# A second attention whose inputs are combined by VectorE alone, with its fillings one tick later

## The chip, the core and the metric
The kernel runs on one core of a Trainium2 chip. The metric is device time in microseconds, the median of three runs. Besides those runs one execution was profiled; all rows below are from it.

## What is computed
A chain of small language-model layers over 8 sequences of 512 tokens, 256 wide: a tower of state-space layers, a window attention, a mixture of experts, a relative attention, a second mixture of experts. The change lies in the relative attention. Cut to what matters:

```python
def _L1_attn_ref(x, Wq, Wk, Wv, Wo, bo, w, v):
    q, k, val = (proj(Wq), proj(Wk), proj(Wv))          # 16 heads of 16
    R = abs(pos[:, None] - pos[None, :])
    R_hat = (1.0 + exp(vv)) / (1.0 + exp(vv - wv * R))
    scores = relu(einsum('bhqd,bhkd->bhqk', q, k)) * R_hat[None]
    scores = where(causal, -inf, scores)
    attn = softmax(scores / sqrt(hd))
    ctx = einsum('bhqk,bhkd->bhqd', attn, val)
    return ctx @ Wo + bo

h = h + _L0_ffn_ref(_layernorm(h), ...)                  # two experts' results a token, weighted
h = h + _L1_attn_ref(_layernorm(h), ...)
```

## The kernel before
The relative attention is one stage (`relative_attention_stage`). Before its own work it has to finish what the experts of the stage ahead left: each token has two result rows, read back from memory, and x must get their weighted sum. Class `Carry` (line 663) does this per sequence b: `load` (SP's queue), `halve` (ScalarE, line 698: one of the two rows times its share), `weigh` (VectorE, line 709, four instructions: the other row times its share, plus the first; line 713: that is added to the bf16 copy `xc`), and `add` (line 718: `xc` is added to x; counted in the semaphore `x_final`). `add` takes the engine as an argument. Sequence 0 is finished in the stage ahead. For sequences 1 to 7 VectorE weighs all seven in a row before the loop, and GpSimd adds each (`C.add(pool, S, b)` in the GpSimd block). The results lie in `turned` (sequences 1, 2 and 7) and in the four slots of the ring `z` (sequences 3 to 6), which the attention uses later.

The attention runs in ticks, one for each of the 8 x 16 heads; `b` is the sequence (a batch of 16 ticks), `i` the tick in it, and `h = 16 b + i`. `drive` (line 1933) writes batch 0 out, loops over batches 1 to 6, and writes batch 7 out with 9 ticks more to drain. There is no scheduler: each engine's function `tick(b, i)` fixes its order, and semaphores join the engines. In tick i:

- TensorE transposes results of earlier heads back (line 2221, in ticks with i % 4 of 3 and 0), computes the four score tiles of head h (line 2234, in the order of `ORDER` = 0, 2, 1, 3), each when VectorE has emptied that bank of the head before; transposes the masked probabilities of head h-3 (line 2246); multiplies by V for four heads at once (line 2261, in ticks with i % 4 of 3, 0 and 1); and then does at most one *filling* of the bank `psum_w` (`fill`).
- VectorE empties the four score tiles (line 2126, multiplied by `rhat`, with maxima), makes `nm` (line 2141), reads the filling of the tick before (`read`), and clamps the exponentials of head h-1 (line 2157), which GpSimd then masks (line 2007).
- ScalarE empties oT (line 2059, i % 4 of 2), reads the filling of the tick before, copies the transposed probabilities to `pt`, a view of `turned` (lines 2068, 2070), and computes the exponentials of head h (line 2076).

A filling is a step of the projections. `PRE` holds those for the next sequence (two sets of transposes "xT", four "qk" and two "v"), `POST` those of the sequence before ("cT" twice, "out" twice). The first number of an entry is its tick. `at_tick(b, i, fill)` ends TensorE's tick i, and the other engines call `at_tick(b, i - 1, read)` in the next. For "qk" ScalarE writes a rounded high part (line 2045) and VectorE the remainder, the low part `lo` (line 2107); for "out" VectorE adds the bank to x (line 2112). A filling waits in `w_free` until the one before has been read. VectorE's read frees the bank, and it stands behind all four score tiles and `nm`. SP's queue stores high and low parts to memory and loads them back as `q_st` and `k_st` for the heads.

Of the kernel before, what the change touches and what calls it, by code (L numbers as in the profile page):

```python
# [24 lines left out]
NB = 8  # L25
# [8 lines left out]
def later(n):  # L34

    return not (isinstance(n, int) and n == 0)
# [1784 lines left out]
def relative_attention_stage(nc, S, A, R, C):  # L1821
# [32 lines left out]
    with ExitStack() as ctx:  # L1854
# [66 lines left out]
        PARTS = [(0, 0), (1, 0), (0, 1), (1, 1)]  # L1921
        PRE = [(1, "xT", 0), (2, "xT", 1), (3, "qk", 0), (4, "qk", 1), (5, "qk", 2), (6, "qk", 3), (7, "v", 0), (8, "v", 1)]
        POST = [(9, "cT", 0), (10, "cT", 1), (11, "out", 0), (12, "out", 1)]

# [67 lines left out]
        def _(pool):  # L1992
            pool.memset(v_now[:, :, :, HV:HC], 0.0)
            pool.memset(vx[:, :], 1.0).then_inc(vones, 1)
            norm.pool_rstd(pool, S.minus_half, 0)
            for b in range(1, NB):
                C.add(pool, S, b)
            pool.wait_ge(loaded, 16 * 5)
# [36 lines left out]
        def _(act):  # L2035
# [17 lines left out]
            def tick(b, i):  # L2053
# [8 lines left out]
                if has(h, 3):  # L2062
                    g = h - 3
                    out = pt[:, (i - 3) % SLOTS, :, :]
                    if has(g, SLOTS):
                        act.wait_ge(o_done, g - 4 - (i - 3) % QUAD)
# [26 lines left out]
        def _(dve):  # L2093
# [24 lines left out]
            def tick(b, i):  # L2118
# [3 lines left out]
                for at, t in enumerate(ORDER):  # L2122
                    if has(h, 0):
                        n = (t + 1) * P
                        dve.wait_ge(s_done, TT * h + FILLED[at]).then_inc(passed, 1)
                        dve.tensor_tensor_reduce(out=z[:, i % RING, t, 0:n], in0=scores[t],  # L2126
                                                 in1=rhat[:, i * T + T - n:(i + 1) * T], scale=1.0, scalar=0.0,
                                                 op0=ALU.mult, op1=ALU.max, accum_out=mx[:, i % 2, t:t + 1]).then_inc(z_ready, 1)
                    half = (i - 3) % QUAD
                    if half < 2 and has(h, 11 + half):  # L2130
# [11 lines left out]
                if i == 0 and (not isinstance(b, int) or b < NB - 1):  # L2142
                    if not later(b):
                        dve.wait_ge(C.x_final, NB)
                    norm.vector_stats(dve, rows_of(b + 1), b + 1)
                if 1 <= i:
                    at_tick(b, i - 1, read)
                if i == 8 and later(b):
# [20 lines left out]
            for use, (_, kind, which) in enumerate(PRE):  # L2169
                read(kind, which, 0, use, FIRST[use])  # L2170
            for b in range(1, NB):
                C.weigh(dve, b, result_at[b])
            drive(dve, tick)
            take_ctx(NB - 1)
# [618 lines left out]
```

## Time and profile before
| | |
|---|---|
| median of 3 runs | 2643.86 us (2642.42 to 2650.0) |
| the profiled execution's own time | 2641.9 us |
| its span | 2640.2 us |
| TensorE busy | 2182.8 us (83%) |
| VectorE busy | 1586.9 us (60%) |
| ScalarE busy | 1325.2 us (50%) |
| GpSimd busy | 744.7 us (28%) |
| mean granted TensorE clock | 0.907 of full |
| relative attention | about 1591 to 2260 us of the span |

Busy shares are over all stages, which have different limits, so they say little of one change. A row of the timeline gives start, duration, engine, line, operation and what is written from what, with the number of instructions merged in it; the bracket is the idle time ahead of it and what ended it. The granted clock of TensorE is 1.00 at 2.4 GHz and 0.50 at 1.2 GHz.

### The profile page before, as it was taken

The page shows a single profiled execution, that of the slowest core. Times are in us where ns is not written, and L with a number is a line of the kernel's source. Part 1 is how long each engine was busy: PE and PEld are TensorE (multiplying, and loading weights), DVE is VectorE, ACT ScalarE, POOL GpSimd, SP SyncE. Part 2 cuts the span into 40 slices and gives each one's busy share as a digit, 9 for nine tenths or more (in the row PEclk, how much of TensorE's full clock was granted, in tenths as well). Part 3 has the DMA queues.
Part 4 walks back from the last instruction along what each step waited for, and adds up shares of the span by engine and source line. Part 5 has one row for each costly group of instructions (what it writes and reads, how often), then busy time and mean ns, then how long its engine had stood idle before and what let it go on. Part 6 is the DMA issues. An engine that isn't in the chain of part 4 may idle for free. (4 is left out here: it accounts for less than half of the span.)

```text
span 2640.2 us, 43175 instructions
## 1 busy us (share of the span) xinstructions
PE 2182.8 (83%) x13073; PEld 1686.4 (64%) x13073; DVE 1586.9 (60%) x4474; ACT 1325.2 (50%) x2652; POOL 744.7 (28%) x835
## 2 busy tenths in 40 slices
PE   3899999999999999767882873888888989695982
PEld 2788888887888888635662651555555556463772
DVE  4555665565556656356764977767777768541225
ACT  2344544454445444345545763867776768210330
POOL 5111111111111111042446662122212222226442
PEclk8899999999999999989986985988989989678996
DMA  5620010000000000022232535222122221303446
GB/s 108 166 33 0 11 33 1 8 13 24 1 8 3 1 1 0 27 65 51 43 64 68 147 109 177 78 67 64 49 70 74 71 69 51 101 33 108 127 137 243
DMA packets 209472, 165.36 MB, mean 63 GB/s; under 512 B 108320, under 2 KB 167376, under 8 KB 209296
## 3 DMA queue, kind: packets, MB, share of 16 engines
q1 hardware_dynamic: 190832, 120.71, 17.3%
q0 software_dynamic: 14240, 38.35, 4.6%
q10 hardware_dynamic: 4224, 4.19, 0.5%
q8 instruction: 81, 1.33, 0.2%
q14 instruction: 95, 0.78, 0.1%
HBM read 91.07 MB, written 72.11 MB: 62 GB/s over the span
## 5 line engine op out<-in xcount | busy, mean ns | idle before, releaser
L630 PE MATMUL psum_o<-w_s,hid_s 128*128 128x256 f32 x3072 | 384.0, 284 | 19.1 <-ACT hid L434 19.1
L616 PE MATMUL psum_h<-xn2T_s,w_s 128*128 128x512 f32 x1536 | 389.9, 404 | 5.4 <-ACT hid L434 3.6
L630 PEld LDWEIGHTS psum_o<-w_s,hid_s 128*128 128x128 f32 x3072 | 371.8, 188 | 27.0 <-issue 19.1
L433 ACT ACTIVATE hid_s<-psum_h,b 128x512 fp32r<-128x512 f32 x256 | 176.5, 689 | 391.5 <-PE psum_h L616 376.0
L616 PEld LDWEIGHTS psum_h<-xn2T_s,w_s 128*128 128x128 f32 x1536 | 283.5, 191 | 87.1 <-ACT hid L434 21.8
L2126 DVE CUSTOM_DVE_ANT_0 ra_z<-ra_psum_s,rhat 128x128 f32<-128x128 f32 (+3 forms) x512 | 224.9, 483 | 132.6 <-PE ra_psum_s L2234 120.5
L2076 ACT ACTIVATE ra_z<-ra_z,ra_nm 128x128 f32<-128x128 f32 (+3 forms) x512 | 245.4, 563 | 0.0
L2007 POOL TENSOR_SCALAR_AFFINE_SELECT ra_z<-ra_z 128x512 f32<-128x512 f32 x128 | 81.6, 637 | 477.3 <-DVE ra_z L2157 477.3
L2246 PE MATMUL ra_psum_p<-ident,ra_z 128*128 128x128 f32 x1280 | 181.4, 293 | 1.3 <-ACT turned L2068 1.3
L517 DVE TENSOR_TENSOR hid_s<-hid,hid_s 128x1024 fp32r<-128x1024 f32 x128 | 156.0, 1223 | 43.1 <-ACT hid L434 42.1
L2068 ACT ACTIVATE turned<-ra_psum_p 128x1024 f32<-128x1024 f32 x128 | 131.3, 1026 | 92.1 <-PE ra_psum_p L2246 92.1
L434 ACT ACTIVATE hid<-psum_h,b 128x512 f32<-128x512 f32 x256 | 174.4, 681 | 0.0
L2246 PEld LDWEIGHTS ra_psum_p<-ident,ra_z 128*128 128x128 f32 x1280 | 148.7, 148 | 35.8 <-issue 35.3
L117 POOL TENSOR_TENSOR ln2n_rstd<-ln2n_var_eps,minus_half 128x4 f32<-128x4 f32 x32 | 32.3, 1009 | 466.1 <-DVE ln2n_var_eps L113 466.1
L2157 DVE TENSOR_SCALAR ra_z<-ra_z,ra_em 128x128 f32<-128x128 f32 (+3 forms) x512 | 162.7, 381 | 0.0
L2234 PE MATMUL ra_psum_s<-ra_k_st,ra_q_st 48*128 48x128 f32 (+3 forms) x512 | 126.1, 367 | 43.1 <-DVE ra_mx L2126 21.2
L600 PE MATMUL psum_y<-ssm_s,xn1T_s 128*128 128x256 f32 x768 | 128.7, 305 | 13.3 <-DVE state L461 13.3
L2234 PEld LDWEIGHTS ra_psum_s<-ra_k_st,ra_q_st 48*128 48x128 f32 x512 | 80.7, 199 | 86.3 <-issue 52.5
L600 PEld LDWEIGHTS psum_y<-ssm_s,xn1T_s 128*128 128x128 f32 x768 | 106.0, 198 | 31.5 <-DVE state L461 16.2
L352 POOL TENSOR_TENSOR x<-x,b 128x1024 f32 (+1 forms) x32 | 101.2, 3162 | 82.1 <-DVE xn L123 70.7
L401 ACT ACTIVATE xn2T_s<-psum_t,ln 128x512 fp32r<-128x512 f32 x64 | 46.4, 775 | 153.5 <-PE psum_t L132 153.5
L117 POOL TENSOR_TENSOR ln1n_rstd<-ln1n_var_eps,minus_half 128x4 f32<-128x4 f32 x32 | 32.6, 1020 | 314.6 <-DVE ln1n_var_eps L113 314.6
(380 smaller groups left out, 4212.4 us busy)
## 6 DMA issues: line engine op xcount, KB each, us to landing
ex_slots<-blank SPq DMA_DIRECT2D x1, 10296.0 KB, 33.8
ex_zT<-ex_slots SPq DMA_DIRECT2D x39, 264.0 KB, 3.0
ex_rows<-ex_slots SPq DMA_DIRECT2D x8, 1056.0 KB, 9.3
w<-in_L_tok_w SPq DMA_DIRECT2D x8, 1024.0 KB, 7.5
ra_scratch<-ra_hi SPq DMA_DIRECT2D x32, 256.0 KB
ra_scratch<-ra_lo SPq DMA_DIRECT2D x32, 256.0 KB
ra_q_st<-ra_scratch SPq DMA_DIRECT2D x128, 64.0 KB, 1.8
ra_k_st<-ra_scratch SPq DMA_DIRECT2D x128, 64.0 KB, 1.8
```

Source lines behind the costliest of these rows:

```text
L433: act.activation(hid_s[:, 0, m, :], psum_h[:, m % 2, :], ACT.Gelu, bias=b1[:, m:m + 1])
L434: act.activation(hid[:, m, :], psum_h[:, m % 2, :], ACT.Gelu, bias=b1[:, m:m + 1]).then_inc(hid_ready, 1)
L517: dve.tensor_tensor(hid_s[:, 1, m:m + 2, :], hid[:, m:m + 2, :], hid_s[:, 0, m:m + 2, :].bitcast(F32), ALU.subtract).then_inc(hid_lo, 1)
L600: pe.matmul(out, xn1T_s[:, parity, x_part, k, tok], ssm_s[:, w_part, SSM_D + k * D:SSM_D + (k + 1) * D], start=(n == 0 and k == 0), stop=F ...
L616: mm = pe.matmul(psum_h[:, m % 2, :], w1_s[:, w_part, k, m * P:(m + 1) * P], xn2T_s[:, x_part, k, :], start=(n == 0 and k == 0), stop=(n = ...
L630: mm = pe.matmul(psum_o[:, t // 2, (t % 2) * D:(t % 2 + 1) * D], hid_s[:, h_part, m, t * P:(t + 1) * P], w2_s[:, w_part, m, :], start=(n = ...
L2068: act.activation(out[:, 0:8, :], psum_p[:, 0:2, :].rearrange("p c (a b) -> p (c a) b", a=4), ACT.Identity).then_inc(pt_act, 1)
L2076: act.activation(z[:, i % RING, t, 0:n], z[:, i % RING, t, 0:n], ACT.Exp, scale=SCALE, bias=nm[:, i % 2, t:t + 1]).then_inc(exp_done, 1)
L2126: dve.tensor_tensor_reduce(out=z[:, i % RING, t, 0:n], in0=scores[t], in1=rhat[:, i * T + T - n:(i + 1) * T], scale=1.0, scalar=0.0, op0=A ...
L2157: last = dve.tensor_scalar(pt_, pt_, em[:, (i - 1) % 2, t:t + 1], None, ALU.max)
L2234: pe.matmul(scores[t], q_st[64 * s:64 * s + 3 * HD, parity, t * P:(t + 1) * P], k_st[64 * s:64 * s + 3 * HD, parity, 0:n], start=True, sto ...
L2246: mm = pe.transpose(psum_p[:, c, a * P:(a + 1) * P], z[:, (i - 3) % RING, q, k * P:(k + 1) * P], S.ident[:, :])
```

## The change
Four edits in the one stage.

1. VectorE does `add` itself, right behind `weigh`, and GpSimd's additions go.
2. Only sequences 1 to 3 are combined ahead of the loop. Sequence 4 follows in tick 0, 5 in tick 1, 6 and 7 in tick 2, behind `nm` (`RESULTS_AT`). VectorE's statistics for sequence 1 wait for `x_final` 2 instead of 8; ScalarE waits for all 8 at tick 3, before it writes into `turned`, and so does VectorE.
3. All fillings stand one tick later (ticks 2 to 13 instead of 1 to 12).
4. VectorE's `at_tick(b, i - 1, read)` is called behind the second score tile, no longer behind `nm`.

```diff
-        PRE = [(1, "xT", 0), (2, "xT", 1), (3, "qk", 0), (4, "qk", 1), (5, "qk", 2), (6, "qk", 3), (7, "v", 0), (8, "v", 1)]
-        POST = [(9, "cT", 0), (10, "cT", 1), (11, "out", 0), (12, "out", 1)]
+        PRE = [(2, "xT", 0), (3, "xT", 1), (4, "qk", 0), (5, "qk", 1), (6, "qk", 2), (7, "qk", 3), (8, "v", 0), (9, "v", 1)]
+        POST = [(10, "cT", 0), (11, "cT", 1), (12, "out", 0), (13, "out", 1)]
+        RESULTS_AT = {0: (4,), 1: (5,), 2: (6, 7)}
...
             norm.pool_rstd(pool, S.minus_half, 0)
-            for b in range(1, NB):
-                C.add(pool, S, b)
             pool.wait_ge(loaded, 16 * 5)
...
                     out = pt[:, (i - 3) % SLOTS, :, :]
+                    if i == 3 and not later(b):
+                        act.wait_ge(C.x_final, NB)
...
                                                  op0=ALU.mult, op1=ALU.max, accum_out=mx[:, i % 2, t:t + 1]).then_inc(z_ready, 1)
+                    if at == 1 and 1 <= i:
+                        at_tick(b, i - 1, read)
...
                 if i == 0 and (not isinstance(b, int) or b < NB - 1):
                     if not later(b):
+                        dve.wait_ge(C.x_final, 2)
+                    norm.vector_stats(dve, rows_of(b + 1), b + 1)
+                if not later(b):
+                    for of in RESULTS_AT.get(i, ()):
+                        C.weigh(dve, of, result_at[of])
+                        C.add(dve, S, of)
+                    if i == 3:
                         dve.wait_ge(C.x_final, NB)
-                    norm.vector_stats(dve, rows_of(b + 1), b + 1)
-                if 1 <= i:
-                    at_tick(b, i - 1, read)
...
-            for b in range(1, NB):
+            for b in range(1, 4):
                 C.weigh(dve, b, result_at[b])
+                C.add(dve, S, b)
             drive(dve, tick)
```

VectorE, from the last results ahead of the loop to the first score tile of tick 0 in batch 0, before:

```order
L709 SCALAR_TENSOR_TENSOR both<-ra_z,both_share 128x256 x4
L713 TENSOR_TENSOR turned<-turned,both 128x1024
L709 SCALAR_TENSOR_TENSOR both<-turned,both_share 128x256 x4
L713 TENSOR_TENSOR turned<-turned,both 128x1024
L2126 ISA ra_z,ra_mx<-ra_psum_s,rhat 128x128
```

and VectorE in the changed kernel, behind the four tiles and `nm` of tick 0 (result 4), up to the tiles of tick 1:

```order
L2144 TENSOR_SCALAR ra_nm<-ra_mx 128x4
L106 BN_STATS ra_n_stats<-x 128x6 x4
L110 BN_AGGR ra_n_mv<-ra_n_stats 128x2 x4
L113 TENSOR_SCALAR ra_n_var_eps<-ra_n_mv 128x4
L709 SCALAR_TENSOR_TENSOR both<-ra_z,both_share 128x256 x4
L713 TENSOR_TENSOR turned<-turned,both 128x1024
L718 TENSOR_TENSOR x<-x,turned 128x1024
L123 TENSOR_SCALAR ra_xn<-x,ra_n_mv,ra_n_rstd 128x256 x4
L2127 ISA ra_z,ra_mx<-ra_psum_s,rhat 128x128
```

The last results moved from ahead of the first tile into the ticks, and each now carries its addition to x (L718).

VectorE in a tick with a low part, in the loop over batches 1 to 6, before (the clamp of the head before, L2157, follows it):

```order
L2126 ISA ra_z,ra_mx<-ra_psum_s,rhat 128x384
L2126 ISA ra_mx 128x1
L2125 REGISTER_ALU
L2126 ISA ra_z,ra_mx<-ra_psum_s,rhat 128x256
L2126 ISA ra_mx 128x1
L2125 REGISTER_ALU
L2126 ISA ra_z,ra_mx<-ra_psum_s,rhat 128x512
L2126 ISA ra_mx 128x1
L2140 ISA
L2141 TENSOR_SCALAR ra_nm<-ra_mx 128x4
L2102 REGISTER_ALU
L2107 TENSOR_TENSOR ra_lo<-ra_psum_w,ra_hi 128x512
```

and in the changed kernel, where the low part has line 2108:

```order
L2127 ISA ra_z,ra_mx<-ra_psum_s,rhat 128x128
L2127 ISA ra_mx 128x1
L2127 ISA ra_z,ra_mx<-ra_psum_s,rhat 128x384
L2127 ISA ra_mx 128x1
L2103 ISA
L2105 REGISTER_ALU
L2108 TENSOR_TENSOR ra_lo<-ra_psum_w,ra_hi 128x512
L2126 REGISTER_ALU
L2127 ISA ra_z,ra_mx<-ra_psum_s,rhat 128x256
```

The low part moved ahead of the third and fourth tile and of `nm`.

TensorE from the transposes of head h-3 to the filling of tick 3 in that loop, before (the first "qk" filling, with Wq):

```order
L2246 MATMUL ra_psum_p<-ident,ra_z 128x128 x10
L2252 ISA
L2261 MATMUL ra_psum_o<-turned,ra_v_now 32x512 x4
L2183 REGISTER_ALU
L2196 MATMUL ra_psum_w<-ra_xnT,ra_wq 128x512 x2
```

and in the changed kernel the same tick, with the second set of transposes of xn as its filling:

```order
L2254 MATMUL ra_psum_p<-ident,ra_z 128x128 x10
L2260 ISA
L2269 MATMUL ra_psum_o<-turned,ra_v_now 32x512 x4
L2191 REGISTER_ALU
L2199 MATMUL ra_psum_w<-ident,ra_xn 128x128 x4
```

The "qk" filling with Wq now ends tick 4, beside the product with V of 384 columns.

## Rows read from the trace of the kernel before

**Rows 1.** Windows (from:to, us; busy PE, PEld, DVE, ACT, POOL; PE clock; DMA; GB/s), batches 1 and 3.
```profile
1710.00:1792.70 82.70, 72.42 (x451) 46.23 (x450) 58.81 (x245) 60.20 (x131) 17.69 (x39) 0.92 0.23 67
...
1872.00:1950.90 78.90, 67.22 (x436) 43.69 (x432) 59.00 (x245) 57.76 (x128) 16.98 (x37) 0.94 0.23 67
```

**Rows 2.** VectorE in order of time (start us, us), results and first ticks.
```profile
1611.10 1.67 DVE L709 SCALAR_TENSOR_TENSOR both<-turned,both_share 128x256 bf16<-128x256 f32 x4 [0.90 <-ACT turned L698]
1612.81 0.69 DVE L713 TENSOR_TENSOR turned<-turned,both 128x1024 bf16<-128x1024 bf16 x1
1613.61 3.56 DVE L709 SCALAR_TENSOR_TENSOR both<-turned,both_share 128x256 bf16<-128x256 f32 x4
...
1639.79 0.28 DVE L2126 CUSTOM_DVE_ANT_0 ra_z<-ra_psum_s,rhat 128x128 f32<-128x128 f32 x1
...
1642.12 1.41 DVE L106 BATCH_NORM_STATS2 ra_n_stats<-x 128x6 f32<-128x256 f32 x4
...
1645.46 1.38 DVE L123 TENSOR_SCALAR ra_xn<-x,ra_n_mv,ra_n_rstd 128x256 f32<-128x256 f32 x4 [1.21 <-POOL ra_n_rstd L117]
...
1648.61 1.27 DVE L2157 TENSOR_SCALAR ra_z<-ra_z,ra_em 128x128 f32<-128x128 f32 x4
...
1653.41 0.29 DVE L2126 CUSTOM_DVE_ANT_0 ra_z<-ra_psum_s,rhat 128x128 f32<-128x128 f32 x1 [0.49 <-PE ra_psum_s L2234]
```

**Rows 3.** Instructions of line 718 and line 709.
```profile
L718 POOL TENSOR_TENSOR x<-x,turned x7: 2119/2123/2132, 1613.6 to 1640.0; 128x1024 f32<-128x1024 f32 x7
L718 DVE TENSOR_TENSOR x<-x,turned x1: 1224/1224/1224, 1589.0 to 1589.0; 128x1024 f32<-128x1024 f32 x1
...
L709 DVE SCALAR_TENSOR_TENSOR both<-ra_z,both_share x16: 471/473/2387, 1618.0 to 1634.3; 128x256 bf16<-128x256 f32 x16
```

**Rows 4.** TensorE in order of time, batch 0.
```profile
1622.77 1.51 PE L2234 MATMUL ra_psum_s<-ra_k_st,ra_q_st 48*128 48x128 f32 x4 [10.47 <-DMA ra_k_st<-ra_scratch]
...
1662.56 1.98 PE L2196 MATMUL ra_psum_w<-ra_xnT,ra_wk 128*128 128x512 f32 x4 [1.25 <-DVE ra_lo L2107]
```

**Rows 5.** Who waited for whom, 1700 to 2240 us.
```profile
PE ra_psum_w L2196 <- DVE ra_lo L2107: 15.9, 18, 1.2
...
PE ra_psum_w L2206 <- DVE x L2112: 5.0, 7, 0.7
...
PE ra_psum_w L2206 <- DVE ra_lo L2107: 2.1, 6, 0.4
```

**Rows 6.** TensorE in order of time, batch 2.
```profile
1825.35 0.90 PE L2234 MATMUL ra_psum_s<-ra_k_st,ra_q_st 48*128 48x128 f32 x4
1826.19 1.31 PE L2246 MATMUL ra_psum_p<-ident,ra_z 128*128 128x128 f32 x10
1828.72 1.98 PE L2196 MATMUL ra_psum_w<-ra_xnT,ra_wk 128*128 128x512 f32 x4 [1.23 <-DVE ra_lo L2107]
...
1857.13 1.99 PE L2206 MATMUL ra_psum_w<-ra_wo,ra_xnT 128*128 128x256 f32 x8 [0.74 <-DVE x L2112]
```

**Rows 7.** VectorE in order of time, batch 2.
```profile
1826.09 0.29 DVE L2126 CUSTOM_DVE_ANT_0 ra_z<-ra_psum_s,rhat 128x128 f32<-128x128 f32 x1 [1.52 <-PE ra_psum_s L2234]
...
1827.98 0.69 DVE L2107 TENSOR_TENSOR ra_lo<-ra_psum_w,ra_hi 128x512 fp32r<-128x512 f32 x1
...
1831.60 0.29 DVE L2126 CUSTOM_DVE_ANT_0 ra_z<-ra_psum_s,rhat 128x128 f32<-128x128 f32 x1 [1.74 <-PE ra_psum_s L2234]
```

**Rows 8.** ScalarE in order of time, batch 2.
```profile
1825.10 0.59 ACT L2059 ACTIVATE ra_oT<-ra_psum_o 128x512 f32<-128x512 f32 x1
1825.58 0.60 ACT L2045 ACTIVATE ra_hi<-ra_psum_w 128x512 fp32r<-128x512 f32 x1
...
1828.60 1.91 ACT L2076 ACTIVATE ra_z<-ra_z,ra_nm 128x128 f32<-128x128 f32 x4
```

**Rows 9.** Busy time by microsecond, batch 1, tick 6.
```profile
1746.00:1747.00 1.00, 0.08 (x1) 0.00 (x0) 0.96 (x4) 1.00 (x2) 0.00 (x0) 1.00 0.00 0
...
1748.00:1749.00 1.00, 1.00 (x2) 0.33 (x1) 0.43 (x2) 1.00 (x2) 0.40 (x1) 0.50 0.00 0
```

## The prediction

> **What bounds the kernel now.** I read the page first: span 2640.2 us, no engine full over the whole of it, so a change is worth what it is worth in its own stage. The relative attention (lines 1830 to 2260) runs from about 1591 to 2260 us. The windows by batch come next: batch 1 takes 82.7 us with TensorE busy 72.4, VectorE 58.8, ScalarE 60.2; batch 3 takes 78.9 with 67.2, 59.0 and 57.8 [rows 1]. The reader is to see that TensorE is the nearest to full and still has a dozen us free in each batch. The table of waits says where part of it goes: the fillings of `psum_w` (the projections, lines 2196 and 2206) wait 15.9 us in 18 cases, and 2.1 in 6, for VectorE's low part of the filling before, and 5.0 in 7 for VectorE's sum into x [rows 5]. That is three and one a batch for batches 1 to 6, and one a batch for the last.
>
> The timeline of one tick shows the ring that closes it. In batch 2, tick 6: VectorE starts its score tiles at 1826.09, reaches the low part only at 1827.98, and waits for its next scores until 1831.60, 1.74 us of it idle [rows 7]. TensorE starts scores at 1825.35 and transposes at 1826.19, would be free for the filling some 1.2 us later, waits 1.23 us for the low part, starts at 1828.72, and only behind that filling come the next scores [rows 6]. So in ticks with a projection both engines wait for each other: VectorE's idle time is behind TensorE, and TensorE's behind the low part. These waits lie on the path.
>
> The other place is the start of the stage. VectorE combines seven results in a row from 1611.10 and reaches the first score tile at 1639.79 [rows 2], though TensorE could give it scores from 1622.77 on, when the keys have landed [rows 4].
>
> **Part 1, combining by VectorE alone.** One result is four weighings, one sum in bf16, and one addition to x. The first time the four take 1.67 us; from the second on they take 3.56 [rows 2], and the four are not all slower: the middle value of one is 0.47 us and the longest 2.39, beside GpSimd's addition of 2.12 [rows 3]. 3.56 less 1.67 is 1.89: one weighing stands still for nearly the length of GpSimd's addition. The Trainium skill (SBUF — State Buffer, Who interferes with whom) says that a VectorE instruction with two SBUF inputs and a GpSimd instruction that reads SBUF exclude each other for the whole instruction; the 1.89 agrees.
>
> On VectorE the addition costs 1.22 (its one case) [rows 3]. A result then costs 2.51 (1611.10 to 1613.61, with the gaps) plus 1.22 and a gap of 0.04, 3.8 us, against 3.56 + 0.69 and gaps, 4.4. Step by step: three results from 1611.10 end at 1622.4; TensorE's first scores start at 1622.77 at the low clock and take 1.51 for four [rows 4]; the first tile needs two of them and a hand-over, so VectorE starts tick 0 at about 1623.9. Tiles and `nm` are 1.8 (1646.84, the end of the normalising, to 1648.61), the statistics 2.1 (1642.12 to 1645.46, less the wait of 1.21): 1627.8. Result 4, 3.8: 1631.6. Normalising 1.4: 1633.0, and GpSimd's power, for which it waited 1.21 [rows 2], is over by then. Tiles 1.8, result 5, 3.8, maxima 1.3: 1639.9. Tick 2: 1.8, results 6 and 7 at 7.6, 1.3: tick 3 at 1650.5, rounded. It starts at 1653.41 now [rows 2]. So the 16 us that tick 0 is earlier are given back in ticks 0 to 2, and **2.9 us** stay.
>
> By the same rule of that page GpSimd's power (1.0 us) would stop a weighing of result 4 that runs beside it. The trace has no such pair. With it 1.9 would stay instead of 2.9.
>
> The added waits: ScalarE waits for all eight additions before it writes the first slot of `pt`; that is tick 3, and the copy stands ahead of its exponentials of tick 3. The additions end at 1649.3, VectorE's tiles of tick 3 only at 1652.3, so it costs nothing. VectorE's own wait at tick 3 is for its own work.
>
> **Part 2, low parts between the score tiles.** The read moves from behind `nm` to behind the second tile. In tick 6 of batch 2 it would start about 0.75 after 1826.09 instead of 1.89 after it [rows 7], 1.1 earlier. The filling then starts when TensorE has done its transposes (and the products with V, where the tick has them). So the waits of rows 5 go nearly whole: (15.9 + 2.1) / 6 = 3.0 a batch for the low parts, and 5.0 / 7 = 0.7 for the sums into x, 3.7 in all.
>
> What is late next: `nm` now stands behind the low part, and so ScalarE's exponentials, and the next high part behind these. The ring through ScalarE: high part 0.60, low part 0.6, last two tiles 1.1, `nm` and em 0.3, exponentials 1.81 [rows 2, 7, 8], with hand-overs 4.4 us, and 0.5 more in the one tick of four that copies oT first [rows 8]. TensorE's own work is 4.3 in tick 6 (5.51 from 1826.09 to 1831.60 [rows 7], less the 1.23) and, as an estimate, about 4.8 to 5.3 in the other ticks with a projection, which hold products with V. So only tick 6 is touched, the one with oT too: at most 4.9 less 4.3, 0.6, at least 0, and I take 0.2, since the longer tick ahead of it lets ScalarE catch up.
>
> **Part 3, fillings one tick later.** The same instructions; what changes is what they share a tick with. The first transposes move from tick 1, where TensorE stood for the normalised rows, to tick 2; but VectorE itself normalises ahead of tick 1's tiles, so tick 2 gains nearly nothing (0.4). Before, the projections began in tick 3, beside the longest product with V; now a second set of transposes (0.7 us at full clock) stands there, and the last `out` filling moves into tick 13, which was light. The light ticks 3 and 11 get short fillings beside long products (about 4.0 us of TensorE by these sums, against 3.1 of VectorE, tiles 1.8 and maxima 1.3). I charge 0.2 a batch for this balance, as a choice between 0 and 1. SP's queue: the second half of the stores of the next batch waits for the last low part, one tick later; behind it stand the loads of the last quad. I cost it at 0, since TensorE's waits from 1700 us on name none for these loads; should they come late, up to 1 us a batch.
>
> A batch thus saves 3.7 - 0.2 - 0.2 = **3.3 us**, six of them 19.8. Batch 7 has only the sum into x: 0.7. Batch 0 has four low waits, the first 1.25 of 1662.56 [rows 4], with two more like it and one of 0.2: 3.8. Against that TensorE now idles before tick 4 of batch 0, since tick 2 is long, and starts the projections at the low clock (1.51 for a tick's four scores against 0.90 [rows 4, 6]): I take 1.5 off, between 0 and 4. Batch 0 then saves 2.9 + 3.8 - 1.5 = 5.2.
>
> Sum: 5.2 + 19.8 + 0.7 = 25.7 us off the profiled execution's 2641.9, 2616.2. The median of the runs is 2643.86, 2.0 above that execution, so the time is **2618 us**. Its own range is 2612 to 2624.
>
> **Rivals.**
> Clock gift. TensorE's clock falls when it pauses: in batch 1, tick 6, it was busy 0.08 of a us at 1746 and the granted clock was 0.50 at 1748 [rows 9]; batch 1 is 3.8 us longer than batch 3 [rows 1]. If closing the pauses keeps the clock up or lets it rise sooner after tick 1, three batches gain some 3 us more: 2643.9 - 35 = 2609. Against: the pause of ticks 0 and 1, where most low stretches start, stays. The Trainium skill (TensorE: Matmul & The Clock Gate, HAM oscillation) likewise puts such falls down to pauses between bursts. Chance 0.15.
>
> Half hidden. The ring through ScalarE costs 0.4 in every projection tick instead of 0.2 once: 28 x 0.4 = 11 less, 2630. For: the hand-overs are summed by me, not seen. Chance 0.12.
>
> Given back. What the heavy ticks save, VectorE and ScalarE, busy 59 and 58 of 79 us, give back in light ticks, 0.5 a batch is left: 2643.9 - 5.2 - 3 = 2636. Against: light ticks already run at VectorE's pace. Chance 0.08.
>
> Not what it says. The weighings stay at 3.56 since something other than GpSimd slows them: 7 results x 1.9 less the one that was fast, 11 us back: 2630. Against: the first of the seven ran free of it with ScalarE busy [rows 2]. Chance 0.05.
>
> Slower: the clock rises later. Ticks 1 to 3 of each batch now hold less of TensorE's work; if its clock stays low two ticks longer, scores, transposes and the product with V (0.90, 1.31 and about 1.0) stretch by 1.51 / 0.90, 2.2 us a tick [rows 4, 6], 7 batches x 4.4 = 31 against 25.7: 2649. It decides if the granted clock is still at half after tick 5 of most batches. Chance 0.04.
>
> **How the numbers follow.** 2618 has 0.56. The range takes in the gift and the half-hidden case: 2608 to 2631; outside remain 0.12 and the tails. This kernel's times tell 0.3% apart, 8 us, so faster means below 2636. Faster: 0.56 + 0.15 + 0.12 + 0.05 = 0.88; same 0.08; slower 0.04.
>
> **What would show it.** Weighings of 1.67 for four throughout; first score tile near 1624, tick 3 near 1650.5; no wait of line 2196's fillings for the low part above 0.3; batches of 75 to 79 us; batch 0 ahead by about 5 at tick 10. Wrong would be: TensorE's fillings waiting for the low part still, VectorE idle before the low part for ScalarE's high part, or granted clock below 0.88 over the batches.

## The result and the profile after

| | before | after |
|---|---|---|
| median | 2646.93 us (4 runs) | 2599.2 us (4 runs, 2594.3 to 2604.82) |
| profiled execution, span | 2641.9, 2640.2 | 2599.22, 2597.5 |
| mean granted clock | 0.907 | 0.914 |
| batches 1 to 6, profiled | 484.5 us | 448.6 us |

The ratio is 0.9819, 95% interval 0.9803 to 0.9836. The forecast was 2618 with 2608 to 2631: the direction is right, but the gain is 47.7 us where 26 were forecast, and the time lies below the range. (The forecast counted from a median of 2643.86; with a fourth run before's median is 2646.93. From 2643.86 the gain would be 44.7.)

The page of the changed kernel, header, busy times and the line of the score tiles:

```profile
span 2597.5 us, 43176 instructions
...
PE 2176.9 (84%) x13073; PEld 1688.5 (65%) x13073; DVE 1583.4 (61%) x4481; ACT 1329.7 (51%) x2652; POOL 728.0 (28%) x828
...
L2127 DVE CUSTOM_DVE_ANT_0 ra_z<-ra_psum_s,rhat 128x128 f32<-128x128 f32 (+3 forms) x512 | 228.7, 483 | 95.0 <-PE ra_psum_s L2242 81.9
```

TensorE's busy time is 5.9 us less, VectorE's 3.5. So nearly all of the gain is idle time. In the last line VectorE's idle time ahead of score tiles is 95.0 us; the same line of before's page has 132.6.

The windows of the same batches 1 and 3 (from:to, us; busy PE, PEld, DVE, ACT, POOL; PE clock; DMA; GB/s), which answer to [rows 1]:

```profile
1706.50:1782.50 76.00, 70.20 (x451) 46.06 (x450) 58.89 (x244) 59.29 (x127) 16.98 (x37) 0.93 0.25 71
1857.50:1932.30 74.80, 67.48 (x432) 44.32 (x432) 58.94 (x245) 58.26 (x127) 16.98 (x37) 0.93 0.25 71
```

Batch 3 is 4.1 us shorter with the same busy time of TensorE (67.5 against 67.2): all of it pause. Batch 1 is 6.7 shorter with TensorE busy 70.2 against 72.4: 2.2 of that is the same work done at a higher clock. Its tick 6, where before's clock fell [rows 9], takes 4.46 us for 7.20. That fall is seen in this one profile only: with the old reads and the old fillings the same tick takes 5.51 and 5.50 in two kernels below (results_only, dve_ahead).

VectorE from the start of the stage (start us, us), which answers to [rows 2]:

```profile
1594.54 1.41 DVE L106 BATCH_NORM_STATS2 ra_n_stats<-x 128x6 f32<-128x256 f32 x4 [1.09 <-PEq L79]
...
1614.30 1.67 DVE L709 SCALAR_TENSOR_TENSOR both<-turned,both_share 128x256 bf16<-128x256 f32 x4 [0.90 <-ACT turned L698]
...
1616.72 1.22 DVE L718 TENSOR_TENSOR x<-x,turned 128x1024 f32<-128x1024 f32 x1
...
1623.86 1.22 DVE L718 TENSOR_TENSOR x<-x,turned 128x1024 f32<-128x1024 f32 x1
1627.98 0.29 DVE L2127 CUSTOM_DVE_ANT_0 ra_z<-ra_psum_s,rhat 128x128 f32<-128x128 f32 x1 [2.90 <-PE ra_psum_s L2242]
...
1631.91 1.67 DVE L709 SCALAR_TENSOR_TENSOR both<-ra_z,both_share 128x256 bf16<-128x256 f32 x4
...
1635.49 1.38 DVE L123 TENSOR_SCALAR ra_xn<-x,ra_n_mv,ra_n_rstd 128x256 f32<-128x256 f32 x4
...
1642.20 1.26 DVE L2164 TENSOR_SCALAR ra_z<-ra_z,ra_em 128x128 f32<-128x128 f32 x4
...
1653.55 0.28 DVE L2127 CUSTOM_DVE_ANT_0 ra_z<-ra_psum_s,rhat 128x128 f32<-128x128 f32 x1
```

The stage's first statistics start at 1594.54, before at 1591.34: 3.2 us later, in work ahead of the change. Counted from there, tick 0 comes at 33.4 (before 48.5), tick 3 at 59.0 (62.1), batch 1 at 112.0 (118.5). The weighings (lowest, median and highest ns, then first and last start), which answer to [rows 3]:

```profile
L709 DVE SCALAR_TENSOR_TENSOR both<-ra_z,both_share x16: 476/477/484, 1621.4 to 1646.4; 128x256 bf16<-128x256 f32 x16
```

Tick 6 of batch 2, TensorE and then VectorE, which answer to [rows 6] and [rows 7]:

```profile
1812.05 0.90 PE L2242 MATMUL ra_psum_s<-ra_k_st,ra_q_st 48*128 48x128 f32 x4
1812.89 1.31 PE L2254 MATMUL ra_psum_p<-ident,ra_z 128*128 128x128 f32 x10
1814.38 1.98 PE L2204 MATMUL ra_psum_w<-ra_xnT,ra_wq 128*128 128x512 f32 x4 [0.18 <-DVE ra_lo L2108]
```

```profile
1812.79 0.29 DVE L2127 CUSTOM_DVE_ANT_0 ra_z<-ra_psum_s,rhat 128x128 f32<-128x128 f32 x1 [1.00 <-PE ra_psum_s L2242]
...
1813.63 0.69 DVE L2108 TENSOR_TENSOR ra_lo<-ra_psum_w,ra_hi 128x512 fp32r<-128x512 f32 x1
1814.24 0.42 DVE L2127 CUSTOM_DVE_ANT_0 ra_z<-ra_psum_s,rhat 128x256 f32<-128x256 f32 x1
...
1817.25 0.29 DVE L2127 CUSTOM_DVE_ANT_0 ra_z<-ra_psum_s,rhat 128x128 f32<-128x128 f32 x1 [0.56 <-PE ra_psum_s L2242]
```

The low part starts 0.84 us behind the first tile (before 1.89), the filling waits 0.18 for it (1.23), VectorE's idle time ahead of the next tick is 0.56 (1.74), and the tick takes 4.46 us (5.51). The waits from 1655 us on (us in total, cases, longest), which answer to [rows 5]:

```profile
DVE ra_z L2127 <- PE ra_psum_s L2242: 79.0, 76, 2.8
...
PE ra_psum_w L2204 <- DVE ra_lo L2108: 1.4, 7, 0.4
```

This stretch takes in batch 0's projections as well. From 1700 us on, the stretch of rows 5, the wait of line 2196's fillings, now line 2204, fell from 15.9 in 18 to 1.1 in 6, none above 0.2.

So, from the two profiles: 6.5 us up to batch 1, 35.9 in batches 1 to 6, 1.0 in batch 7, 43.4 in the stage. Against that stand the later start of 3.2 and 2.5 gained behind the stage, neither of them part of the change: 42.7 between the spans.

### The profile page after: what moved, and what is told of

The parts are those of the page before. It is cut to its first block and busy times, and to the rows that moved or that the text cites. A ratio compares the mean times of both kernels' runs of the same rounds, so it can differ in the third digit from the quotient of the medians.

```text
span 2597.5 us, 43176 instructions
## 1 busy us (share of the span) xinstructions
PE 2176.9 (84%) x13073; PEld 1688.5 (65%) x13073; DVE 1583.4 (61%) x4481; ACT 1329.7 (51%) x2652; POOL 728.0 (28%) x828
## 5 line engine op out<-in xcount | busy, mean ns | idle before, releaser
L2127 DVE CUSTOM_DVE_ANT_0 ra_z<-ra_psum_s,rhat 128x128 f32<-128x128 f32 (+3 forms) x512 | 228.7, 483 | 95.0 <-PE ra_psum_s L2242 81.9
L117 POOL TENSOR_TENSOR ln1n_rstd<-ln1n_var_eps,minus_half 128x4 f32<-128x4 f32 x32 | 32.6, 1019 | 315.5 <-DVE ln1n_var_eps L113 315.5
```

## The experiments

All ratios are against the kernel before on the same chip. The runs below fell on four chips, on which it takes 2704.23, 2645.15, 2649.39 and 2703.41 us; kernels of different chips are compared by ratios, and by lengths in their profiles. A batch is counted from its first score tile to that of the next. "Late" is a batch in which the low stretch of TensorE's clock lasts 10 us or more behind the start of tick 1. In the thirteen profiles of kernels without added transposes and without an edit at the head of the loop the clock came back 5.0 to 7.2 us behind that start in 48 batches and 10.7 to 12.3 behind it in 30, and never in between. The lengths of batches are from one profile each, and a profile is one execution: those of read_only and results_only were 6.5 and 5.5 us above the median of their runs, those of before, fill_only, results_read and results_fill 5 to 8 below.

| kernel | fillings | reads | results | ratio, 95% | batches 1 to 6 | late |
|---|---|---|---|---|---|---|
| before | old | old | old | 1 | 484.5 | 4 |
| results_only | old | old | new | 0.998 (0.9962 to 0.9998) | 487.9 | 5 |
| read_only | old | new | old | 0.9864 (0.9832 to 0.9897) | 461.3 | 4 |
| fill_only | new | old | old | 0.9905 (0.9876 to 0.9934) | 468.6 | 1 |
| results_read | old | new | new | 0.9904 (0.9882 to 0.9927) | 468.3 | 6 |
| fill_read | new | new | old | 0.9845 (0.982 to 0.9869) | 447.5 | 0 |
| results_fill | new | old | new | 0.9913 (0.9882 to 0.9943) | 468.4 | 0 |
| after | new | new | new | 0.9819 (0.9803 to 0.9836) | 448.6 | 1 |
| after, again | new | new | new | 0.9811 (0.9782 to 0.984) | 448.6 | 1 |

### One part alone

Again: the changed kernel, unaltered, where before takes 2704.23.

> The changed kernel unaltered, for a second profile and a firmer ratio. Both theories expect 43 to 50 us faster than before. Theory of the moved fillings (the clock is back at full in tick 2 of batches 2 to 6 because of the new order): the profile again shows batches 4 to 6 at 75 us, tick 3 at 3.9 us. Theory of chance (where the low-clock stretch ends is luck): some of these batches take 2 to 3 us more, with tick 3 at 5 to 6 us.

2654.12 against 2704.23 us. The ratio is that of the first comparison, and so is the profile of the batches.

The other three take one part each from the change:

```diff
fill_only, against before
+        PRE = [(2, "xT", 0), (3, "xT", 1), (4, "qk", 0), ...]
+        POST = [(10, "cT", 0), (11, "cT", 1), (12, "out", 0), (13, "out", 1)]
read_only, against before
+                    if at == 1 and 1 <= i:
+                        at_tick(b, i - 1, read)
...
-                if 1 <= i:
-                    at_tick(b, i - 1, read)
results_only, against after
+        PRE = [(1, "xT", 0), (2, "xT", 1), (3, "qk", 0), ...]
+        POST = [(9, "cT", 0), (10, "cT", 1), (11, "out", 0), (12, "out", 1)]
...
-                    if at == 1 and 1 <= i:
-                        at_tick(b, i - 1, read)
...
+                if 1 <= i:
+                    at_tick(b, i - 1, read)
```

> The kernel before with only the fillings one tick later. Theory of the waits alone (the gain is TensorE's waits for the low part and nothing else): within 4 us of before, since each low part still stands behind nm. Theory of the moved fillings: the low-clock stretch of batches 1 and 4 to 6 ends in tick 2 instead of tick 3, 2.5 us each, so 8 to 12 us faster.

> The kernel before with only the low parts (and the sums into x) between the score tiles. Theory of the waits alone: about 26 us faster (3.7 in each of batches 1 to 6, 3.8 in batch 0), and nearly all of the gain of the whole change less 3. Theory of the moved fillings: 20 to 26 us faster too, but tick 3 of batches 4 to 6 stays at 7 us, so that the whole change is more than the sum of its parts' waits.

> The kernel before with only the results: VectorE adds, four of seven spread over ticks 0 to 2. Both theories: 3 us faster, tick 3 of batch 0 starts 3 us earlier against the start of the stage; tick 0 16 us earlier. If the port were not the reason for the weighings of 3.56 us, they would stay so and nothing would be gained.

2677.21, 2672.27 and 2700.63 against 2704.23. The moved reads take 23.2 us out of the six batches and leave 4 late; their waits for low parts fall to 1.8 us in 8 (from 1690 us on). The moved fillings, which I had charged with 0.2 a batch, take 15.9 out and leave 1 late, though the wait that I thought to be all the gain stays, in the waits of fill_only from 1690 us on:

```profile
PE ra_psum_w L2196 <- DVE ra_lo L2107: 14.8, 20, 1.2
```

Its stage starts 25.9 us later than before's; in the stretch that answers to rows 5 (1726 to 2266) it is 13.3 us in 18 cases, before 15.9 in 18.

### Two parts, and the third back

```diff
fill_read, against after: seven results ahead of the loop, added by GpSimd
-                    for of in RESULTS_AT.get(i, ()):
-                        C.weigh(dve, of, result_at[of])
-                        C.add(dve, S, of)
results_read, against after
+        PRE = [(1, "xT", 0), (2, "xT", 1), (3, "qk", 0), ...]
+        POST = [(9, "cT", 0), (10, "cT", 1), (11, "out", 0), (12, "out", 1)]
results_fill, against after
-                    if at == 1 and 1 <= i:
-                        at_tick(b, i - 1, read)
...
+                if 1 <= i:
+                    at_tick(b, i - 1, read)
```

> Fillings later and low parts early, the results as before. If the parts add up: the whole change less 3 us, so 40 to 45 us faster than before.

> The changed kernel with the fillings at their old ticks. Theory of the waits alone: 3 us or less slower than the whole change. Theory of the moved fillings: 10 to 15 us slower than the whole change, with tick 3 of batches 4 to 6 at 6 to 7 us at the low clock.

> The changed kernel with VectorE's reads back behind nm; results spread and fillings late. From the profiles of the parts: batches of 78 us, the low part waited for in every projection tick; 15 to 20 us slower than the changed kernel, about 0.988 of before.

2604.38 and 2620.07 against 2645.15; 2680.93 against 2703.41. The table now has every combination. The moved reads are worth 23.2, 19.6, 21.1 and 19.8 us over the six batches, 3.3 to 3.9 a batch, whatever stands beside them (before to read_only, results_only to results_read, fill_only to fill_read, results_fill to after). The moved fillings are worth 15.9, 13.8, 19.5 and 19.7, 2.3 to 3.3 a batch (before to fill_only, read_only to fill_read, results_only to results_fill, results_read to after). With the results as the change has them, taking either back costs 0.9% of the time. The ratios of the times, which don't hang on one execution, have the same sign in all four pairs but spread more: the moved reads bring 1.36, 0.76, 0.60 and 0.94%, the moved fillings 0.95, 0.19, 0.67 and 0.85%, and the 0.19 (read_only to fill_read) is within the intervals. The results bring little in any company, and beside the moved reads alone they cost: 0.9904 for 0.9864, with 6 batches late for 4.

Where the fillings' gain lies is seen in single ticks. VectorE's first tile of tick 3 and of tick 4 in batch 4: before, results_read, after.

```profile
1968.27 0.29 DVE L2126 CUSTOM_DVE_ANT_0 ra_z<-ra_psum_s,rhat 128x128 f32<-128x128 f32 x1 [1.37 <-PE ra_psum_s L2234]
...
1975.71 0.29 DVE L2126 CUSTOM_DVE_ANT_0 ra_z<-ra_psum_s,rhat 128x128 f32<-128x128 f32 x1 [4.16 <-PE ra_psum_s L2234]
```

```profile
1946.01 0.29 DVE L2127 CUSTOM_DVE_ANT_0 ra_z<-ra_psum_s,rhat 128x128 f32<-128x128 f32 x1 [1.37 <-PE ra_psum_s L2242]
...
1953.27 0.29 DVE L2127 CUSTOM_DVE_ANT_0 ra_z<-ra_psum_s,rhat 128x128 f32<-128x128 f32 x1 [3.97 <-PE ra_psum_s L2242]
```

```profile
1949.25 0.29 DVE L2127 CUSTOM_DVE_ANT_0 ra_z<-ra_psum_s,rhat 128x128 f32<-128x128 f32 x1 [0.57 <-PE ra_psum_s L2242]
...
1953.13 0.29 DVE L2127 CUSTOM_DVE_ANT_0 ra_z<-ra_psum_s,rhat 128x128 f32<-128x128 f32 x1 [0.60 <-PE ra_psum_s L2242]
```

Tick 3 takes 7.44, 7.26 and 3.88 us, and VectorE's idle time at its end is 4.16, 3.97 and 0.60. TensorE's granted clock, in single microseconds, first results_read and then after:

```profile
1949.00:1950.00 1.00, 1.00 (x8) 0.00 (x0) 0.29 (x1) 1.00 (x5) 0.54 (x1) 0.50 0.40 137
1951.00:1952.00 1.00, 1.00 (x4) 0.44 (x3) 0.00 (x0) 0.59 (x1) 0.00 (x0) 1.00 0.19 51
```

```profile
1947.00:1948.00 1.00, 1.00 (x6) 1.00 (x5) 0.96 (x6) 1.00 (x2) 0.00 (x0) 0.50 0.00 0
1949.00:1950.00 1.00, 1.00 (x9) 0.75 (x8) 0.75 (x5) 1.00 (x3) 0.68 (x2) 1.00 0.00 0
```

At 1949 both kernels are in tick 3 (it began at 1946.0 and 1949.3); results_read stands at 0.50 (1.2 GHz), after at 1.00 (2.4 GHz). The clock had come back in tick 2 of after, 5.9 us behind the start of tick 1, and in results_read 11.7 behind it, some 4 us into tick 3.

Between results_read and after the batches are shorter by 0.9, 3.2, 3.9, 3.5, 3.4 and 4.9. The first is the one in which after's clock rises late too. In the others ticks 2 to 4 alone give 4.2 to 4.6, and batches 2 to 5 give 0.6 to 1.2 of it back elsewhere. Where the clock rises early under the old fillings as well, the moved fillings bring little: batches 2 and 5 of read_only take 75.12 and 75.40, those of fill_read 74.95 and 74.93. With the old reads it is somewhat more: batches 2 and 3 of before take 79.30 and 78.86, those of fill_only 77.98 both. The late batches 3 and 4 of read_only take 78.52 and 78.07 against 74.74 and 75.19.

### Is it the place of the transposes?

```diff
transposes_old, against after
+        PRE = [(1, "xT", 0), (2, "xT", 1), (4, "qk", 0), (5, "qk", 1), ...]
warm_old, against results_read; warm_new, against after
+                    pe.wait_ge(w_free, uses(b))
+                    for n in range(count):
+                        pe.transpose(psum_w[:, 0:P], rhat[:, 0:P], S.ident[:, :])
```

The last two add 34 transposes whose output nobody reads, in three places of tick 1, where TensorE stands idle.

> The changed kernel, but the two transposing fillings of xn stay at ticks 1 and 2; all other fillings are late as in the change, tick 3 has none. Theory A (the low-clock stretch lasts into tick 3 because TensorE restarts with a filling in tick 1): the clock is at half until 11 to 12 us after the start of tick 1 in most of batches 2 to 6. Theory B (the place of the heavy filling is what matters): the stretch is as long, but tick 3 takes 4 to 5 us instead of 7.3, since nothing heavy lies in it, and the batch takes 75 to 76 us, 1 us more than in the changed kernel at most. Theory C (chance): stretches of both lengths.

> The changed kernel with the fillings at their old ticks, and 34 more transposes of rhat into the free bank psum_w in tick 1 of batches 1 to 6, in TensorE's pauses (their results are not used). If the low clock in ticks 1 to 3 costs the 2.6 us a batch: clock full in tick 3, tick 3 at 5.2 us instead of 7.2, batches at 75 to 76 us instead of 78.4. If the place of the fillings costs it whatever the clock: no gain.

> The changed kernel with the same 34 added transposes (results not used). The low clock costs little there, ticks 2 and 3 take 3.4 to 4.1 and 3.9 us: at most 1 us a batch faster, or up to 1 us slower a batch if the transposes run over the pauses.

Transposes back in ticks 1 and 2: 2597.86 against 2649.39, 0.9819 (0.9795 to 0.9843), 448.6 us, 1 late. My theory that TensorE must work longer without the transposes ahead of the rise falls: their place doesn't decide. Which of the other fillings does, no run separates, since the "qk" and "v" fillings and those of `POST` ("cT", "out") moved together in every kernel. The last of `POST` stand in tick 13 instead of 12, near the end of the batch before.

The added transposes: warm_old 2625.1, 0.99 (0.987 to 0.993), 465.4 us, 5 late; warm_new 2599.4, 0.9815 (0.9794 to 0.9835), 448.7 us. The added work mostly did not bring the clock back early under the old fillings: it came 11 us behind the start of tick 1 in batches 1 and 4 to 6, and in batch 3 it was full through ticks 1 and 2 and low from 6.6 to 10.0 us, in tick 3. It did not fill every pause either: in batch 4 TensorE still stood for 1.68 us around the start of tick 1, and the low stretch began 1.2 us behind that start. In warm_old's batch 2 the clock was back early, and VectorE's tick 3 there shows what an early rise alone gives:

```profile
1804.33 0.29 DVE L2127 CUSTOM_DVE_ANT_0 ra_z<-ra_psum_s,rhat 128x128 f32<-128x128 f32 x1 [0.39 <-PE ra_psum_s L2251]
...
1809.55 0.29 DVE L2127 CUSTOM_DVE_ANT_0 ra_z<-ra_psum_s,rhat 128x128 f32<-128x128 f32 x1 [1.93 <-PE ra_psum_s L2251]
```

5.22 us, as in before's batches 2 and 3 (5.20, 5.21), and the batch takes 75.62. So an early clock gives about 2 us in tick 3. In warm_new the clock was higher for longer (mean over the span 0.922) and the time the same. Batches 1, 4 and 5 had the full clock through ticks 1 and 2 and took 72.78, 74.24 and 74.18 us, for after's 76.00 (late), 74.87 and 75.26. Against that batches 2 and 6 were late, and took 77.53 and 75.34. So a full clock in ticks 1 and 2 is worth 0.6 to 1.1 us more than an early rise, and one late rise takes back more than that.

### Does the length of a batch set it?

```diff
longer_1 (tick 10) and longer_2 (ticks 2 and 10), against after
+                if i in (2, 10) and later(b) and (not isinstance(b, int) or b < NB - 1):
+                    for n in range(3):
+                        dve.tensor_scalar(pad[:, n * D:(n + 1) * D], rhat[:, 0:D], 1.0, None, ALU.mult)
```

> The changed kernel with three more instructions on VectorE (copies of 128x256 of rhat into an unused tile) in the light tick 10 of batches 1 to 6: 0.9 us more work a batch. Theory of separate terms (the low stretch falls where it falls): each batch 0.9 us longer, 5 us in all. Theory of stepping (the end of the low stretch moves in steps, and a batch's length with it): the batches keep their 75 us or jump to 78, so the sum is 0 or well over 5 us, and no batch lies at 76.

> The same three instructions in ticks 2 and 10: 1.8 us more a batch. Separate terms: batches at 76.7, 11 us in all. Stepping: batches at 75 and at 78 us, few between.

2653.23, 0.9821 (0.9782 to 0.986), 449.2 us, 1 late; 2657.76, 0.981 (0.9769 to 0.9852), 452.3 us, 2 late. Inconclusive: the added work lengthened tick 10 by less than expected (3.08 to 3.66 us), and tick 11 gives half of that back (3.53 to 3.23), so a batch grew by 0.3 us and not by 0.9. In longer_2 batch 6 went late and took 75.82 for 72.7. That is a price of 3.1 us for a late rise under the new fillings, but not a proof of what causes it.

### The additions on VectorE, all ahead of the loop

```diff
dve_ahead, against before
             for b in range(1, NB):
                 C.weigh(dve, b, result_at[b])
+                C.add(dve, S, b)
```

GpSimd's additions are gone too.

> The kernel before, only with VectorE adding instead of GpSimd, all seven results still ahead of the loop. Port theory: each weighing of four takes 1.67 us, a result 3.6 instead of 4.4, tick 0 starts 4 to 5 us earlier and the kernel is 4 us faster. If another reason slows the weighings (ScalarE's halving, the slots of z), they stay at 3.56 and the kernel is 5 us slower.

2647.24, 1.0007 (0.9993 to 1.0021). The weighings:

```profile
L709 DVE SCALAR_TENSOR_TENSOR both<-ra_z,both_share x16: 476/476/477, 1621.4 to 1633.3; 128x256 bf16<-128x256 f32 x16
```

None stood still, and tick 3 is 4.0 us earlier in the stage (58.1 against 62.1). The run is not faster all the same: in its profile the six batches took 2.9 more (487.4), and in that of results_only 3.4 more, though neither edit touches them. Most of this lies in one place, tick 0 of batches 2 to 6, and not in late rises. VectorE there, in batch 3, before and dve_ahead:

```profile
1874.21 0.69 DVE L2126 CUSTOM_DVE_ANT_0 ra_z<-ra_psum_s,rhat 128x512 f32<-128x512 f32 x1 [0.94 <-PE ra_psum_s L2234]
```

```profile
1873.57 0.42 DVE L2124 CUSTOM_DVE_ANT_0 ra_z<-ra_psum_s,rhat 128x256 f32<-128x256 f32 x1 [1.50 <-PE ra_psum_s L2233]
```

VectorE waits for scores within tick 0 in both, but 0.9 to 1.2 us ahead of the fourth tile where GpSimd adds (before, read_only, fill_only, fill_read), and 1.4 to 1.7 ahead of the third where VectorE adds (after and all the others that loop). The tick takes 9.7 to 10.0 us in the first group and 10.2 to 10.5 in the second (power_first, below, apart), with no batch between. Over the five batches that is 2.0 of dve_ahead's 2.9 and 2.4 of results_only's 3.4. Why it depends on this edit stays open; when the batches are written out (below) the wait is gone. What the part alone is worth is 0 to 0.4% of the time.

### What is left: the head of the loop and GpSimd's power

```diff
power_first, against after, in GpSimd's tick, ahead of its mask
+                if i == 0 and (not isinstance(b, int) or b < NB - 1):
+                    norm.pool_rstd(pool, S.minus_half, b + 1)
...
-                if i == 0 and (not isinstance(b, int) or b < NB - 1):
-                    norm.pool_rstd(pool, S.minus_half, b + 1)
unrolled, against after: batches 1 to 6 written out
-            with eng.Fori(1, NB - 1) as b:
+            for b in range(1, NB - 1):
...
-                if later(b):
+                if later(b) or use >= len(PRE):
```

unrolled_pf has both.

> The changed kernel with GpSimd's power of tick 0 ahead of its mask. VectorE waits 2.0 us in each of six batches for the power, which stands behind the mask. Theory that this wait is on the path: 2 us a batch, 12 us faster than the changed kernel. Theory that the next score tiles of TensorE are as late: 0 to 3 us.

> The changed kernel with batches 1 to 6 written out instead of looped, and GpSimd's power of tick 0 ahead of its mask. If the 2.4 us that VectorE stands at the head of the loop and the 2.0 us for the power are on the path: 4 us a batch, some 20 to 25 us faster than the changed kernel, near 0.972 of before. If TensorE's scores are as late: 0 to 5 us.

> The changed kernel with batches 1 to 6 written out, GpSimd's power behind its mask as before. If the loop's head costs its 2.4 us: 12 to 14 us faster than the changed kernel, 0.977 to 0.978 of before; if only together with the earlier power does it count: 0 to 5 us.

power_first 2595.52, 0.9804 (0.9776 to 0.9832): the batches 441.7, 6.9 less, but batch 7 took 4.7 more: TensorE's clock was low in it for 6.8 and for 3.4 us, and in after's batch 7 not at all. The time is after's within the intervals. unrolled 2632.09 against 2703.41, 0.9737 (0.9706 to 0.9768), batches 434.2. unrolled_pf 2586.83 against 2649.39, 0.976 (0.9736 to 0.9783), batches 429.8, and batch 7 again with two low stretches and 3.2 us longer than in unrolled; 0.972 had been expected. Both written-out kernels beat before and the changed kernel. By the ratios of after, again (0.9811), and of unrolled, writing out is worth 0.74%, an estimated 20 us of 2703, and 14.4 of that is seen in batches 1 to 6 of the profiles. VectorE at the head of batch 3, in after and in unrolled:

```profile
1857.50 0.29 DVE L2127 CUSTOM_DVE_ANT_0 ra_z<-ra_psum_s,rhat 128x128 f32<-128x128 f32 x1 [2.38 <-issue]
...
1859.78 0.42 DVE L2127 CUSTOM_DVE_ANT_0 ra_z<-ra_psum_s,rhat 128x256 f32<-128x256 f32 x1 [1.47 <-PE ra_psum_s L2242]
```

```profile
1883.09 0.29 DVE L2127 CUSTOM_DVE_ANT_0 ra_z<-ra_psum_s,rhat 128x128 f32<-128x128 f32 x1
...
1890.44 1.38 DVE L123 TENSOR_SCALAR ra_xn<-x,ra_n_mv,ra_n_rstd 128x256 f32<-128x256 f32 x4 [2.00 <-POOL ra_n_rstd L117]
```

"issue" is time in which VectorE waited for nothing that the profile shows: 2.38 us when the loop turns, and none where the batches are written out. The wait of 1.47 us within tick 0 goes too: the tick takes 8.65 for 10.30. The 2.00 for the power stay; the last kernel takes its place at the head of GpSimd's tick, and tick 0 falls from 8.65 to 7.19.

## Why the prediction was wrong

**What bounds.** Right: the ring of low part, filling and next scores, and the start of the stage. The windows of batch 3 show the same TensorE work in 4.1 us less.

**Part 1.** Right up to tick 3, and short of one cost behind it. Tick 0 came 33.4 us into the stage (1623.9 as I put it would be 32.6), tick 3 3.07 us earlier than before (2.9); a result took 3.58 us where my sum has 3.8, which made up for the later tick 0. The step "one weighing stands still for nearly the length of GpSimd's addition" is shown by dve_ahead and by the row of weighings of after: highest 477 and 484 ns for 2387. The case that the weighings stay slow is out. What the part is worth in the time of all is small (0.998): tick 0 of batches 2 to 6 became 0.5 us longer, 2.4 in all, which no term of the forecast has, and which takes back most of the 2.9. GpSimd's power, for which I had an alternative of 1.9, ran beside a weighing of result 4, at 1631.91 on VectorE:

```profile
1632.14 1.12 POOL L117 TENSOR_TENSOR ra_n_rstd<-ra_n_var_eps,minus_half 128x4 f32<-128x4 f32 x1 [34.02 <-DVE ra_n_var_eps L113]
```

The four weighings took 1.67 as ever, the power 1.12 where it takes 1.02 alone, the same in all thirteen profiles with such a pair. By the Trainium skill (SBUF — State Buffer, Who interferes with whom) a VectorE instruction with two SBUF inputs and a GpSimd instruction that reads SBUF shut each other out. By that rule one weighing should have stood still for about the power's length; here the trace does not agree, for an instruction of four columns, though for GpSimd's addition of 2.12 it did. The added wait of ScalarE did last (4.64 us at 1652.48, ended by the last addition) and cost nothing, since `nm` of tick 3 came 1.7 us later still.

**Part 2.** Right. 3.7 less 0.2 a batch was forecast; the four pairs of kernels give 3.3 to 3.9. Ticks 4, 6 and 12 fell from 5.81, 5.51 and 5.59 to 4.77, 4.46 and 4.78. In tick 6 0.18 was left where I took 0.2, as a wait for the low part. "Half hidden" and "given back" are out.

**Part 3: the step that failed.** "The same instructions; what changes is what they share a tick with ... I charge 0.2 a batch for this balance." The four pairs give a gain of 2.3 to 3.3 a batch in its place, 14 to 20 us over six; against the forecast's loss of 1.2 that covers the 16.1 us by which batches 1 to 6 beat their 19.8. (By the times themselves it is less exact, 0.19 to 0.95%, an estimated 5 to 25 us.) I summed tick 3 at full clock ("short fillings ... about 4.0 us of TensorE by these sums") and did not ask at which clock tick 3 runs. In before it runs mostly at half clock in four batches of six: its 7.44 us in batch 4 against 5.21 in batch 2 stood in the trace. At one clock the sum was nearer: early against early the moved fillings bring 0.2 to 0.5 beside the new reads, and 0.9 to 1.3 beside the old.

**The rivals.** The clock gift had the direction and 0.15: "if closing the pauses keeps the clock up or lets it rise sooner after tick 1". Its mechanism is wrong in half. The moved reads close the pauses, and their kernels leave 4 and 6 of 6 late. It is the moved fillings that let it rise sooner: where the projections begin in tick 3, 23 of 30 batches are late (before, results_only, read_only, results_read, dve_ahead); where they begin in tick 4, 7 of 48 (both runs of after, fill_only, fill_read, results_fill, transposes_old, longer_1, longer_2). The four kernels that have the new order and an edit at the head of the batch as well (warm_new, power_first, unrolled, unrolled_pf) are late in 9 of 24, so the order alone doesn't settle it. Its size was near for what it names: from before to after three batches, 4 to 6, turn from late to early and are 6.7 to 7.0 us shorter, where 2 and 3, early in both, are 4.4 and 4.1 shorter. What its 2609 lacks, 10 us, lies mostly elsewhere: batch 1 gains 6.8, of which some 1.7 is the fall in its tick 6 that only this profile of before has, and batches 2 and 3 gain 0.8 to 1.1 more than the 3.3 of the sum. "The clock rises later", put down for a slower kernel, is the same step with the wrong sign.

**Batch 0.** 6.5 us for 5.2 (6.1 ahead at tick 10, where about 5 was named). Behind tick 3 that is 3.4 for 3.8 less 1.5, so the 1.5 taken off for a low clock at its projections was too much. Batch 7: 1.0 for 0.7.

**Open.** Why the clock comes back some 6 us earlier when the projections begin in tick 4. The rise lies in tick 2, ahead of both places; ticks 1 and 2 hold the same work in results_read and in transposes_old. So it hangs on something further back: the last fillings of the batch before ("out" in tick 13 for 12), or the start of the low stretch (about 5 us ahead of tick 1, or 1 behind it, in most late batches, about 7.5 ahead in most early ones). The batches cluster: about 75, 78.4 and 82 us. That is what I would try next; no run here separates where the low stretch starts from how much work stands around it.

## What to carry to other kernels

Before an edit moves heavy TensorE work from one tick to the next, look up the granted clock of both ticks in each repetition: the tick with the first projection took 7.4 us in a low stretch and 5.2 outside it, and here the order that kept it out also let the clock rise sooner. Compare repetitions of one loop body with each other first; where they differ by some per cent (here 78.9 and 81.9 us), a state outside the instructions is at work, and it can be worth as much as the wait that one set out to remove (2.6 to 3.4 us a batch against 3.3 to 3.9). And price each part of a change by kernels with every combination of them, in ratios to a common one: the part that seemed neutral carried 14 to 20 of the 36 us that six batches gained, and the part whose own sum came out right brought almost nothing, since a tick that no edit touches had become longer.

## What the runs showed of the hardware

- The clock of TensorE came back either about 6 (5.0 to 7.2) or about 12 us (10.7 to 12.3) behind the start of tick 1, in batches of one kernel with the same instructions; a late rise cost 2.6 (81.90 against 79.30 in before) to 3.4 us (78.52 against 75.12 in read_only) under the old fillings, and 1.9 (tick 3 of after's batch 1, 5.78 for 3.88) to 3.1 under the new.
- 34 transposes in the idle time of tick 1 left it low in tick 3 in five of six batches under the old fillings.
- A turn of the loop over registers stood for 2.1 to 2.5 us of "issue" on VectorE, and a further wait of 0.9 to 1.7 us came within the next tick; written out, both were gone and the six batches took 14.4 us less in the profiles.
- GpSimd's power of 128x4 beside a weighing with two inputs from SBUF stopped no weighing (1.67 us for four, the power 1.12 for 1.02); beside GpSimd's addition of 128x1024 one weighing took 1.9 us more.
